# Eight experts on one core: scaled inputs made by features, their weights spread to all partitions through DRAM

## The reference

```python
scores = sigmoid(xt @ gate.T)
_, sel = top_k(scores + expert_bias, 2)            # two of eight experts for each token
routed = xt[token_idx] * scores_sorted[:, None]    # the input scaled by the expert's score
xb = routed.astype(bfloat16)
for e in range(8):
    h = silu(xb @ w1e.T) * (xb @ w3e.T)            # 512 -> 256 features, bf16 weights
    out_r += where(expert_ids == e, h @ w2e.T, 0)  # 256 -> 512
hs = silu(xt @ shared_w1.T) * (xt @ shared_w3.T)   # a shared expert in f32
out = hs @ shared_w2.T; out = out.at[token_idx].add(out_r)
x = layernorm(x + out)
```

## Time and profile before

| what | value |
|---|---|
| median of 3 runs | 3180.47 us (3171.82 to 3184.24) |
| profiled execution, its own time | 3184.6 us |
| its span | 3182.8 us |
| TensorE busy over the span | 2906.7 us (91%) |
| VectorE busy | 2040.1 us (64%) |
| ScalarE busy | 1546.9 us (49%) |
| GpSimd busy | 1064.0 us (33%) |
| experts stage, from its first up-projection to its last output | 2843.86 to 3178.25 us of the span |

### The profile page before, as it was taken

One profiled execution on the slowest core, in us unless ns is written; L12 is line 12 of the kernel. 1 busy time (PEld: TensorE's weight loads), 2 busy tenths in 40 slices (PEclk: granted clock), 3 DMA queues, 4 the chain that ended last, 5 costly groups with the idle time before them and its releaser, 6 DMA issues. The chain is left out here.

```text
span 3182.8 us, 51969 instructions
## 1 busy us (share of the span) xinstructions
PE 2906.7 (91%) x19232; PEld 1918.3 (60%) x19232; DVE 2040.1 (64%) x2555; ACT 1546.9 (49%) x2949; POOL 1064.0 (33%) x951
## 2 busy tenths in 40 slices
PE   7999799888888888879999899999979899989998
PEld 5666356444444444446666777777756565667776
DVE  4788666699999999661110299999997232324444
ACT  3444212398999899641111366666663111114333
POOL 0000044366666566420000167788884000000000
PEclk9999799799999999889999999999988999989999
DMA  2011322288888789630003111111122600200000
GB/s 90 28 33 34 101 73 79 66 170 163 168 171 168 158 167 196 162 133 27 22 17 128 47 47 54 54 54 54 47 87 78 119 27 20 67 20 27 20 20 27
DMA packets 497993, 256.63 MB, mean 81 GB/s; under 512 B 412160, under 2 KB 449664, under 8 KB 496256
## 3 DMA queue, kind: packets, MB, share of 16 engines
q1 hardware_dynamic: 487504, 247.66, 30.7%
q0 software_dynamic: 10288, 6.29, 1.4%
HBM read 121.65 MB, written 33.69 MB: 49 GB/s over the span
## 5 line engine op out<-in xcount | busy, mean ns | idle before, releaser
L1107 DVE TENSOR_REDUCE xh_top<-xh_seen 128x1 f32<-128x512 f32 (+1 forms) x768 | 632.0, 864 | 49.8 <-PE xh_seen L1009 36.2
L1079 ACT ACTIVATE xh_prob<-xh_sc,xh_bias,xh_scale 128x1024 int16<-128x1024 f32 (+1 forms) x512 | 610.0, 1201 | 72.9 <-PE xh_sc L1009 72.8
L2238 POOL TENSOR_TENSOR ss_state<-ss_du,ss_b_all 128x1024 f32<-128x1024 f32 x128 | 437.5, 3430 | 193.3 <-PE ss_turned L1812 118.0
L1009 PE MATMUL xh_seen<-xh_kT,xh_qT 96*128 96x512 bf16 x1024 | 358.2, 392 | 78.0 <-DVE xh_top L1107 75.5
L2286 DVE TENSOR_TENSOR_SCAN ss_state<-ss_decay,ss_state 128x1024 f32<-128x1024 f32 x128 | 386.0, 3016 | 29.5 <-ACT ss_decay L2090 29.4
L1009 PE MATMUL xh_sc<-xh_kT,xh_qT 96*128 96x512 bf16 x1024 | 314.0, 389 | 1.3 <-ACT xh_prob L1079 1.3
L1133 POOL CAST xh_probT<-xh_pairs 128x2048 int16<-128x2048 uint8 x128 | 241.8, 1889 | 12.7 <-DMA xh_pairs<-xh_prob 4.0
L1009 PEld LDWEIGHTS xh_seen<-xh_kT,xh_qT 96*128 96x128 bf16 x1024 | 90.2, 98 | 241.0 <-DVE xh_top L1107 217.5
L1819 PE MATMUL ss_bank<-ss_xc,hold_w_conv 128*128 128x256 f32 x1024 | 229.3, 379 | 0.7 <-ACT ss_xc L2102 0.7
L2090 ACT ACTIVATE ss_decay<-ss_delta,ss_a 128x255 f32<-128x255 f32 x512 | 210.9, 496 | 1.1 <-DVE ss_state L2286 0.7
L1819 PEld LDWEIGHTS ss_bank<-ss_xc,hold_w_conv 128*128 128x128 f32 x1024 | 190.0, 189 | 26.4 <-ACT ss_xc L2102 1.1
(11 more groups left out here) (306 smaller groups left out, 5025.4 us busy)
## 6 DMA issues: line engine op xcount, KB each, us to landing
ss_b_all<-ss_states SPq DMA_DIRECT2D x8, 2048.0 KB, 7.1
xa_kT<-xp_kT SPq DMA_DIRECT2D x8, 768.0 KB, 5.9
xh_qT<-xa_qT SPq DMA_DIRECT2D x48, 128.0 KB, 3.3
xh_kT<-xa_kT SPq DMA_DIRECT2D x48, 128.0 KB, 3.4
sa_x<-in_x SPq DMA_DIRECT2D x8, 512.0 KB, 3.8
sa_y<-in_x SPq DMA_DIRECT2D x8, 512.0 KB, 4.6
x_after_self_attention<-sa_y_out SPq DMA_DIRECT2D x8, 512.0 KB, 3.0
xp_x<-x_after_self_attention SPq DMA_DIRECT2D x8, 512.0 KB, 6.6
```

The costliest lines, as they stand in the source:

```text
L1009: ins = pe.matmul(out[:, c * D:(c + 1) * D], qT[s][:, t * P:(t + 1) * P], kT[s][:, at + c * D:at + (c + 1) * D], start=True, stop=True)
L1079: act.activation(out, scores, ACT.Exp, bias=bias[t % RING][:, :], scale=scale[s][:, t:t + 1], accum_out=total[s][:, half, t:t + 1]).then_i ...
L1107: ins = v.tensor_reduce(top[t % RING][:, k:k + 1], scores[:, 0:n], AX.X, ALU.max)\
L2238: g.tensor_tensor(state[k % RING][:, :, :], du[s][:, :, :], spread(b_all[s][:, k, :], KD), ALU.mult)\
```

## The change

Nothing is changed outside `experts`. An expert's scaled input is no longer made with tokens on partitions and then transposed; it is made at once with features on partitions, from `xT`. There the weight of a token varies along the row, and is the same on all partitions. So the weights of a batch, 16 numbers (two token tiles, eight experts) on each of 128 partitions, are written to DRAM (8 KB), and all 2048 of them are read back to every partition (`everywhere`, two transfers of 512 KB). In `everywhere` the 16 numbers of one partition lie together, so the weights of one expert for successive tokens are 16 f32 numbers apart. `scaled` is one operation of 128x1024 with two f32 inputs. TensorE no longer turns anything for each expert, ScalarE copies no turned input. The next batch's input is turned and routed at the start of the step, in banks of its own (`xin`), `xT` is doubled, and the choice of experts is made in two parts, after `hid(1)` and `hid(2)`. SP's loop is written out, with the weights' transfers in it.

```diff
+    RING = 4
...
-        ident_b = p.sb("ident_b", [P, P], BF16)
-        xT = p.sb("xT", [P, KD, S])
+        xT = [p.sb(f"xT{s}", [P, KD, S]) for s in (0, 1)]
...
-        xe = [p.sb(f"xe{i}", [P, TB, D], BF16) for i in (0, 1)]
-        xeT = [p.sb(f"xeT{i}", [P, KD, S], BF16) for i in (0, 1)]
+        everywhere = [p.sb(f"everywhere{s}", [P, P, TB * E]) for s in (0, 1)]
+        xeT = [p.sb(f"xeT{i}", [P, KD, S], BF16) for i in range(RING)]
...
-        tp = [p.ps(f"tp{i}", [P, KD, S], BF16) for i in (0, 1)]
+        xin = [p.ps(f"xin{i}", [P, D]) for i in range(TB)]
+        w_dram = nc.dram_tensor("ex_weights", [2, P * TB * E], F32, kind="Internal").ap()
...
+            def weights(n):
+                slot = w_dram[n % 2:n % 2 + 1, :]
+                sp.wait_ge(chosen, ONE + n + 1)
+                if n >= 1:
+                    for i in (0, 1):
+                        sp.wait_ge(w_here[i], ONE + 16 * n)
+                sp.dma_start(slot.rearrange("o (p e) -> (o p) e", p=P), flat(weight[:, :, :])).then_inc(w_out, 16)
+                sp.wait_ge(w_out, ONE + 16 * (n + 1))
+                if n >= 2:
+                    sp.wait_ge(xe_ready, ONE + (n - 1) * E)
+                for i in (0, 1):
+                    half = P * TB * E // 2
+                    sp.dma_start(everywhere[n % 2][:, i * P // 2:(i + 1) * P // 2, :].rearrange("p a e -> p (a e)"),
+                                 slot[:, i * half:(i + 1) * half].to_broadcast([P, half])).then_inc(w_here[i], 16)
+
+            load_x(sp, 1, 1)
+            weights(0)
+            for n in range(B):
+                if n + 1 < B:
+                    weights(n + 1)
+                if n + 2 < B:
+                    sp.wait_ge(x_free[n % 2], ONE + n // 2 + 1)
+                    load_x(sp, n + 2, n % 2)
+                sp.wait_ge(y_done, ONE + n + 1)
+                sp.dma_start(tokens(x_out, n), y_out[n % 2][:, :, :]).then_inc(stored[n % 2], 16)
...
-                for t, bank in enumerate((up1[1], up3[1])):
+                pe.wait_ge(r_exp, ONE + n)
+                for t, bank in enumerate(xin):
                     for c in range(KD):
-                        ins = pe.transpose(bank[:, :, :].rearrange("p k s -> p (k s)")[:, c * P:(c + 1) * P],
-                                           x[s][:, t, c * P:(c + 1) * P], ident[:, :])
+                        ins = pe.transpose(bank[:, c * P:(c + 1) * P], x[s][:, t, c * P:(c + 1) * P], ident[:, :])
...
-                def turn(e):
+                to_features(pe, up1[0], s1, 0, xT[s], KH)
+                to_features(pe, up3[0], s3, 0, xT[s], KH).then_inc(up_ps, 1)
+
+                def expand(e):
 
                     pe.wait_ge(xe_ready, ONE + n * E + e + 1)
-                    pe.wait_ge(tp_sb, ONE + n * E + e - 1) if e >= 2 else pe.wait_ge(tp_sb, ONE + n * E)
-                    transpose_tokens(pe, tp[e % 2], xe[e % 2], ident_b).then_inc(tp_ps, 1)
-
-                def expand(e):
-
-                    pe.wait_ge(tp_sb, ONE + n * E + e + 1)
...
-                    to_features(pe, up1[j], w1[:, e * KD:(e + 1) * KD, :], 0, xeT[e % 2], KH)
-                    to_features(pe, up3[j], w3[:, e * KD:(e + 1) * KD, :], 0, xeT[e % 2], KH).then_inc(up_ps, 1)
+                    to_features(pe, up1[j], w1[:, e * KD:(e + 1) * KD, :], 0, xeT[e % RING], KH)
+                    to_features(pe, up3[j], w3[:, e * KD:(e + 1) * KD, :], 0, xeT[e % RING], KH).then_inc(up_ps, 1)
...
-                turn(0)
-                turn(1)
+                if more:
+                    turn_input(n + 1, 1 - s)
                 for e in range(E):
                     expand(e)
-                    if e + 2 < E:
-                        turn(e + 2)
-                    if e == E - 1 and more:
-                        pe.wait_ge(hid_ready, ONE + n * UPS + E)
-                        turn_input(n + 1, 1 - s)
+                    if e == 0 and more:
+                        route(n + 1, 1 - s)
                     contract(e - 1)
-                if more:
-                    route(n + 1)
                 contract(E - 1)
...
-            act.activation(ident_b[:, :], ident[:, :], ACT.Copy).then_inc(ident_ready, 1)
...
+            def odds(n):
                 act.wait_ge(r_ps, ONE + n + 1)
-                act.activation(flat(score[:, :, :]), up1[1][:, 0, 0:TB * E], ACT.Exp, scale=-1.0).then_inc(r_exp, 1)
+                act.activation(flat(score[:, :, :]), xin[0][:, 0:TB * E], ACT.Exp, scale=-1.0).then_inc(r_exp, 1)
...
-                copy_turned(0)
-                copy_turned(1)
+                if more:
+                    front(n + 1, 1 - s)
...
+                    if e == 0 and more:
+                        odds(n + 1)
...
+            def choose_second(n):
+                chain = Chain(v, chain_s, 6, n)
+                best_of(chain, picked)
                 chain(v.tensor_tensor(pick[:, :, :], pick[:, :, :], picked[:, :, :], ALU.add))
-                chain(v.tensor_tensor(weight[:, :, :], pick[:, :, :], score[:, :, :], ALU.mult))
+                v.wait_ge(w_out, ONE + 16 * n)
+                v.tensor_tensor(weight[:, :, :], pick[:, :, :], score[:, :, :], ALU.mult).then_inc(chosen, 1)
                 chain.end()
...
-                v.wait_ge(tp_ps, ONE + n * E + e - 1) if e >= 2 else v.wait_ge(tp_ps, ONE + n * E)
-                for t in range(TB):
-                    ins = v.tensor_scalar(xe[e % 2][:, t, :], x[s][:, t, :], weight[:, t, e:e + 1], None, ALU.mult)
-                ins.then_inc(xe_ready, 1)
+                if e == 0:
+                    for i in (0, 1):
+                        v.wait_ge(w_here[i], ONE + 16 * (n + 1))
+                by_token = everywhere[s][:, :, :].rearrange("p a (t e) -> p e t a", e=E)[:, e:e + 1, :, :]
+                four = lambda a: a[:, :, :].rearrange("p k (t a) -> p k t a", t=TB)
+                v.tensor_tensor(four(xeT[e % RING]), four(xT[s]), by_token.to_broadcast([P, KD, TB, P]), ALU.mult)\
+                    .then_inc(xe_ready, 1)
...
+                    if more and e == 1:
+                        choose(n + 1)
+                    if more and e == 2:
+                        choose_second(n + 1)
                 if more:
-                    choose(n + 1)
+                    v.wait_ge(xT_sb, ONE + n + 2)
                     scaled(n + 1, 1 - s, 0)
                     scaled(n + 1, 1 - s, 1)
...
             choose(0)
+            choose_second(0)
+            behind.late_vector(v)
+            v.wait_ge(xT_sb, ONE + 1)
             scaled(0, 0, 0)
             scaled(0, 0, 1)
-            behind.late_vector(v)
```

68 lines of the change are left out of this document (24 added, 44 removed).

## The result

The changed kernel takes 3165.93 us (median of 5 runs, 3162.28 to 3168.04), the kernel before, run beside it, 3179.73. The ratio is 0.9959, with a 95% interval of 0.9941 to 0.9978: 14 us or 0.4% shorter, a small difference but clear of none. In a second comparison it was 3164.61 against 3178.28 (0.9954, 0.9938 to 0.9971). Nearly all of it must come from the experts stage, the only one that was touched, so I first read the same view as in the earlier trace rows, busy time by stretches: one row for each batch (the last cut off 1.2 us before its end) and their sum. It runs 313.7 us, from 2842.57 to the last output at 3156.24, and took 334.4 before.

A forecast was written before the change was run, and what follows sets the result against it. TensorE was taken to bound the experts stage (busy 315.9 of 334.4 us). Start -0.3, batch 0 +9.0, six batches -10.7, last -5.5, clock +6.3 gave -1.2 us: median 3179, forecast's own range 3165 to 3196, for all 3150 to 3210.

The forecast's parts named there:

- x: Length of each expert's new VectorE scaling product: 2.1 us, between 1.23 and 3.02; total moves 45 us per microsecond.
- the wait for the next input: TensorE behind each steady batch's shared up-projection: a new wait of 2x - 2.3, as two scalings precede the residual sum.
- the clock: Granted clock falls after the seven in-loop routings, 1.8 us each: none would give back 12.6 us; half, 6.3, taken.
- Batch 0: First batch: weights go through DRAM unhidden, expert 0 starts at 2864.1 instead of 2855.96; 52.3 us against 43.3, 9.0 lost.
- Above x = 1.86 VectorE leads: Per expert while VectorE still scales: its slot of x + 0.75 exceeds TensorE's 2.61 us above this x.
- 4(x + 0.75): VectorE's chain through experts 2 to 5 of a steady batch, each slot x, 0.69 hidden product and 0.06 between.
- 6x + 26.9: Steady batch, one shared up-projection to the next: 39.5 us at x = 2.1 instead of 41.3; six save 10.7.
- The last batch: Final batch, with no turn, routing or choice: 37.9 us against 43.4, 5.5 saved.
- Exchange hidden: Steady batches: weights chosen just after hid(2) have 12.7 us until hid(7), for 7.5 of DMA.
- The first: Rival: the scaling product's stepped read runs at full rate, x = 1.23; 28.9 us shorter, 3152; chance 0.23.
- The second: Rival: steps cost much more, x of 2.5 to 3.0, VectorE becomes the bound; 3206 at x = 2.7; chance 0.30.
- The third: Rival: weights arrive late each batch, landing at 15 us instead of 7.5; stall 2.3 per batch, 3195; chance 0.04.

The follow-up runs named there:

- read in order: Changed kernel with the scaling product reading the spread weights in order, not 16 words apart (tokens get each other's weights): 3149.7 us, 0.9906 to the kernel before.
- the last kernel: Changed kernel with choice early, first exchange ahead, residual sum first, and weights laid down expert by expert in DRAM, read in order: 3146.6 us, 0.9892 to the kernel before.
- weights first: Changed kernel with batch 0's weights and the second input sent ahead of the previous stage's last output on SyncE's queue: 3152.6 us, 0.9912 to the kernel before.
- in four: Changed kernel with each expert's scaling product cut into four over 256 elements each: 3171.9 us, 0.9969 to the kernel before.
- choice early: Changed kernel with the whole choice of the next batch's experts ahead of expert 1's hidden product on VectorE: 3148.4 us, 0.9905 to the kernel before.
- narrow no idle: Changed kernel with the sixteen narrow routing products done a second time, right behind the down-projection before the last, waiting for nothing: 3169.7 us, 0.9959 to the kernel before.
- the combined one: Changed kernel with choice early, batch 0's weights and second input ahead in the queue, and residual sum before the two scalings: 3138.1 us, 0.9875 to the kernel before.
- the one with narrow products after the idle time: Changed kernel with the sixteen narrow routing products done again behind the idle 0.55 us before the last down-projection: 3184.0 us, 1.0019 to the kernel before.

## Why the prediction was right, and where not

The forecast was 3179 us, no change to be told. Measured were 3165.9, inside the range of 3150 to 3210 and 0.9 us inside the forecast's own 3165 to 3196. With 0.41% the difference falls within the 0.5% that I called the same; but I also wrote that 16 us can't be told from none, and the interval (0.2 to 0.6% shorter) does tell these 14. So the answer held, and by little: the sum was off in x, in the wait for the next input and in the clock, all in one direction. Between the two traced executions the kernel is 21.9 us shorter where the sum said 1.2.

- **Batch 0, right in its mechanism, its number luck.** Weights at hand 2862.0 (measured 2862.1), expert 0 at 2864.1 (2864.06), 52.3 us (52.32). But the weights left 1.4 us earlier than forecast (2853.3 for 2854.7) and their store took 3.4 for 2.1. Expert 0 started 21.5 us into the batch for 20.6, and the rest took 30.8 for 31.7. And the clock's return behind the idle stretch differs: in five other kernels with the same exchange the same batch took 54.9 to 58.3 us (in two of them with 1.8 of added work), in one 50.4.
- **x, mis-sized.** "One row has the operation and the other the length of a slow pass, and neither has the stepping; being no nearer to one, I take the middle, x = 2.1." It is 1.89. By my slope of 45 that is 9 us, by the measured 4.4 per batch some 6. The slow pass was a recurrence, and no evidence on steps; the nearest row in kind was the product in order.
- **"Above x = 1.86 VectorE leads", failed.** I added busy times end to end, x + 0.75, where consecutive operations overlap by about 0.08 each. The turn is 2.40 at x = 1.89 and 2.60 at 2.08, so VectorE never led, and of the four turns in 4(x + 0.75) only those of experts 2 and 3, with the choice between them, follow x. The only hint that I had was in my own text of batch 0, where four scalings of 480 ns are "overlapping, 1.7 less".
- **The wait for the next input, mis-sized.** This is where the steady batches came out shorter than 6x + 26.9, 38.2 at the measured x, for 37.2 to 37.6. In batch 3 (37.15 us) it is 0.46 us instead of the 1.5 of 2x - 2.3: the two scalings overlap with what follows (0.3), the load landed in 3.6 us instead of 4.1, and the shared product, under which it hides, took 7.07 instead of 6.8. The chain from expert 1 to down-projection 7 gave only 0.3 more (20.85 for 21.2). The end at x = 1.23 (35.5 us) was good: 35.1.
- **Clock, half wrong.** I took half of the falls to remain. None did, 5.4 us in the six batches. What the prediction named as against them, that the idle 0.4 us is gone, is borne out by 61 sets of narrow products without idle time and without a fall; put back, it brought falls in some batches only.
- **The last batch**, 37.3 for 37.9, 6.0 saved for 5.5.
- **Exchange hidden, right.** In batch 2 the spread is issued at 2958.3, and its median landing is 4.4 us; the scalings that need it start at 2968.55, 5.8 us after it has landed.

The six middle batches took 224.0 us, for 237.0 and 5.4 of clock forecast: 18.4 less. 7.6 of that is x by the prediction's own slope, 5.4 the clock, and of the last 5.4 nearly all is the input's wait (3.7 us in the six batches for 8.9 by the formula). The rivals: none occurred as written. The first (3152) had its mechanism tested by the read in order: 3149.7, with batches of 35.1 for 35.5, but also a batch 0 of 56.4 for 49.2 and one fall for half of seven, so that the total agrees by offsets. The second is excluded up to x = 2.08: VectorE's turn only reaches TensorE's there, and the time is 3171.9; a longer x was not tried. The third's late weights did not come (1.45 and 4.4 us for the 7.5); where the store was slow, 10.5 us in the last kernel, a steady batch took no longer, with the choice made earlier.

What stays open: the stage is 20.7 us shorter in the traces and the medians differ by 13.8. The traced execution of the kernel before is 4.9 us above its median, that of the changed one 3.2 below (5.5 in its second trace), so the traces show a slow one of the first and fast ones of the second. Against the changed kernel, five variants (read in order, weights first, in four, choice early, narrow no idle) come out 8 to 11 us better by the ratios than by their stages. That fits a batch 0 nearer 56 than 52 in the untraced executions of the changed kernel; it was not shown. In seven of the other kernels the stage's difference to before and the median's lie within 4 us of each other; in the combined one they are 47 and 40, in the one with narrow products after the idle time -3 and +6. Open, too, is what decides how long the clock stays low behind the first idle stretch, and whether it falls at all.

## What to carry to other kernels

Work that leaves the bounding engine brings only what the next chain lets through: here 39 us of TensorE's busy time became 21 of the stage. New waits took the rest: for an exchange queued behind a store (8.3 us in batch 0), for sixteen small operations placed where a product was due (1.8 us per batch), and for an input freed late (0.6). Each of these was a matter of order, and putting them right brought 26 us by the medians, more than the change itself (14). Look for the idle stretch of the engine that is given new work, and place the chain of small operations there; and don't shorten an operation whose engine has stopped being waited for.

## What the runs showed of the chip that I had not expected

- Two neighbouring f32 words and then a step of 16: 1.217 us for 1024 elements, as in order; one word and a step of 16: 1.89.
- A DRAM store of 8 KB in pieces of 4 bytes: the read that waits for it is issued 10.5 us behind it. In pieces of 64 bytes: 1.45.
- 0.4 to 0.55 us of idle TensorE and then sixteen products of 8 columns were followed by a fall of the granted clock, as to the 0.54 of the earlier trace rows, in some cases: seven of seven in the kernel before, two of seven and two of twelve in others. The same products with no idle time in front never were (61 cases), nor four of them behind the idle time (seven).
- Behind 3.3 idle microseconds TensorE's clock was at half speed for 10.2 us, behind two idle stretches of 4.5 to 7.7 us each for 10.2 to 20.5 in eight traces; in the combined kernel, behind 3.0, it did not fall, and expert 0's up-projections took their full-clock 1.92 us.
